# The rows of gathers between two waits of GpSimd: three rows of five against one of seven and one of eight

## The chip, the core and the metric

The kernel runs on one core of a Trainium2 chip. Its time is the device time of one launch in microseconds (us). The engines are PE (TensorE), with its weight loads as PEld, DVE (VectorE), ACT (ScalarE), POOL (GpSimd) and SP (SyncE, which only issues transfers here). Each has its own instruction stream; they meet in semaphores alone.

## What is computed

A recommendation tower for 2048 samples. Each sample has 32 ids, one per field; each id picks a row of 16 f32 values out of its field's table. The products of every pair of the 32 rows are summed to 496 numbers, 16 dense values are appended, and a small network follows:

```python
e = jnp.stack([tbl_0[ids[:, 0]], ..., tbl_31[ids[:, 31]]], axis=1)
z = jnp.sum(e[:, row, :] * e[:, col, :], axis=2)      # all pairs row < col
h = jnp.concatenate([z, dense_ctx], axis=1)
h = jnp.maximum(h @ W_top1 + b_top1, 0.0)             # 512 x 512
h = jnp.maximum(h @ W_top2 + b_top2, 0.0)             # 512 x 256
y = h @ W_top3
```

Seventeen tables have 1000 or 1250 rows; fifteen have 12,500 or 125,000.

## The kernel before

The samples go in 16 tiles of 128, one sample per partition. For the 17 small tables PE looks the rows up: a one-hot matrix times the table, split in three bf16 parts, in six rounds for each tile; DVE picks the result out of PSUM (`pick`, line 470). The one-hots come from ACT (`distances` at line 844, `onehots` at line 854), out of a block of group numbers, `gids`, which SP loads for each tile as a broadcast to 128 partitions (line 297, 17 x 128 f16 values or 4352 bytes in each partition).

The 15 large tables can't be looked up so. For them POOL issues 15 gathers per tile (line 367), each an indirect DMA that brings one field's row of 16 values for all 128 samples. The fields stand in three groups of 7, 5 and 3, and each group has a semaphore for even and one for odd tiles, `landed[g][t % 2]`; every gather adds 16 to it when its data has landed.

In its window for tile t, DVE

- multiplies the small fields among themselves (`small_products`, line 480),
- waits for group 0 and multiplies its 7 fields with the 17 small ones (line 489, 128x1904), and then with each other (line 498),
- waits for group 1 and does the same (line 489, 128x1920), and sums part of the products (line 517),
- waits for group 2 (line 489, 128x1392, and line 508) and sums the rest (line 517).

Between these it does the six picks of tile t+1. PE sums the first 384 pairs by transposes (line 663), turns what DVE has summed (line 670) and runs the network for tiles t-1 and t-2 (lines 683, 692 and 699), with ACT's copies between its steps (line 882 is the copy of z to SBUF, which is layer 1's input).

What sets the order around the change:

- POOL's stream is written out, with no loop. It first builds a few constants, and then does nothing but the 240 gathers and their waits. From tile 2 on, POOL may write a group of tile t only after DVE has used the same group of tile t-2 (semaphore `made`).
- POOL also waits for its own gathers. The 15 fields of a tile are numbered 0 to 14 (`place`), and after places 4, 9 and 14 it waits until the gathers of that group issued so far have landed, before it issues the next one. In the last tile there is no such wait.
- SP's stream is a chain of waits: for tile t it waits until ACT has used the `gids` of tile t-1, loads those of tile t+1 (line 297), waits until the z of tile t-2 is complete in PSUM, and loads the dense values of tile t (line 301). So the next load of `gids` also stands behind that wait for z.

The loops of DVE, PE, ACT and SP take two tiles in one round; tiles 0, 1, 14 and 15 are written apart.

Of the kernel before, what the change touches and what calls it, by code (L numbers as in the profile page):

```python
# [28 lines left out]
S = len(SMALL)  # L29
# [23 lines left out]
GROUPS = [7, 5, 3]  # L53
GROUP_AT = [S + sum(GROUPS[:g]) for g in range(len(GROUPS) + 1)]

RUN = 5

SHIFTS = (S - 1) // 2
CIRCLES = [(GROUPS[0] - 1) // 2, (GROUPS[1] - 1) // 2, 0]
# [55 lines left out]
def dlrm_tower(nc, dense, ids, small_ids, ids_dram, tables, w1, b1, w2, b2, w3, out):  # L115
    with ExitStack() as ctx:
# [3 lines left out]
        def sem(name):  # L120
            return ctx.enter_context(nc.semaphore(name))
# [91 lines left out]
        landed = [[sem(f"landed{g}_{i}") for i in range(2)] for g in range(len(GROUPS))]  # L213
# [42 lines left out]
        LAST_TILE = TILES - 1  # L256

        def steps_done(t, step):
            return STEPS * t + step + 1
# [78 lines left out]
        @block.gpsimd  # L338
        def _(pool):
            nc.gpsimd.iota(row_int[:], pattern=[[1, 1]], base=0, channel_multiplier=1).then_inc(iotas_made, 1)  # L340
            nc.gpsimd.iota(cand_int[:], pattern=[[1, SLOTS]], base=0, channel_multiplier=0).then_inc(iotas_made, 1)
            nc.gpsimd.iota(field_int[:], pattern=[[1, TENS], [0, SLOTS]], base=0, channel_multiplier=0
                           ).then_inc(iotas_made, 1)
            nc.gpsimd.iota(place_int[:], pattern=[[1, TENS * SLOTS]], base=0, channel_multiplier=0
                           ).then_inc(iotas_made, 1)
            nc.gpsimd.memset(ident[:], 0.0).then_inc(ident_zeroed, 1)
            pool.wait_ge(ident_zeroed, 1)
            nc.gpsimd.affine_select(out=ident[:], in_=ident[:], compare_op=ALU.not_equal, fill=1.0, base=0,
                                    pattern=[[-1, P]], channel_multiplier=1).then_inc(ident_ready, 1)

            pool.wait_ge(first_ids_loaded, 16)
            for t in range(TILES):
                if t == 1:
                    pool.wait_ge(ids_loaded, 16)
                for g, n in enumerate(GROUPS):
                    if t >= 2:

                        pool.wait_ge(made, steps_done(t - 2, GROUP_STEPS[g]))
                    for i in range(n):
                        f = FIELDS[GROUP_AT[g] + i]  # L360
                        at = (PLACES[g] + i) * D
                        done = landed[g][t % 2]
                        if t == LAST_TILE:
                            for k, (group, first, count) in enumerate(LAST_PIECES):
                                if group == g and first <= i < first + count:
                                    done = last_landed[k]
                        nc.gpsimd.indirect_dma_start(  # L367
                            emb[:, t, at:at + D], None, tables[f],
                            bass.IndirectOffsetOnAxis(ap=idx[:, t, f:f + 1], axis=0)
                        ).then_inc(done, 16)  # L370
                        place = GROUP_AT[g] + i - S
                        if t < LAST_TILE and place % RUN == RUN - 1:
                            pool.wait_ge(done, 16 * (t // 2 * n + i + 1))

        @block.vector
        def _(dve):
# [653 lines left out]
```

## Time and profile before

| | us |
|---|---|
| time, median of 3 runs | 390.6 (388.05 to 390.77) |
| time of the profiled execution | 392.31 |
| its span, first to last instruction | 390.5 |
| PE busy | 301.6 (77%) |
| DVE busy | 248.0 (63%) |
| POOL busy | 227.9 (58%) |
| ACT busy | 145.0 (37%) |

The mean granted clock of TensorE was 0.921. The times of launches are what is compared; the span is the part of a launch that the trace shows. A row of the timeline gives start, duration, engine, line, operation, output and input, the count where rows were merged, and in brackets how long the engine had been idle before it and what ended that idle time ("issue" is nothing that the profile shows). The bar of POOL's row ends where it has written out the gather's work list, not where the data has landed.

### The profile page before, as it was taken

The numbers are of one execution on the slowest core, as the hardware profiler recorded it, in microseconds if no ns is written. First come the engines' busy times: TensorE is split into PE (matmuls) and PEld (weight loads), VectorE is DVE, ScalarE is ACT, GpSimd is POOL, SyncE is SP. The second block draws the span as 40 slices with busy tenths as digits, with TensorE's granted clock in tenths as the row PEclk, the third lists the DMA queues.
The fourth block names the chain that finished last, engine by engine and source line by source line (L and its number), as shares of the span: only waits on it lengthen the run. The fifth ranks groups of instructions, "written<-read, shape, count | busy, mean of one in ns | idle before, by whom it ended". The sixth has DMA issues, their size and how long they took to land.

```text
span 390.5 us, 7439 instructions
## 1 busy us (share of the span) xinstructions
PE 301.6 (77%) x2748; PEld 278.9 (71%) x2748; DVE 248.0 (63%) x326; ACT 145.0 (37%) x311; POOL 227.9 (58%) x250
## 2 busy tenths in 40 slices
PE   1658697999777967977796797879679786978377
PEld 1348696888776857977785797768579776877366
DVE  6798769565956567394647739464673946556541
ACT  3982443434442424344242434424243441113012
POOL 6446655566656656665665666566566656657700
PEclk9988899899998999889899988989998898999759
DMA  6770020202020200102030110202012000000000
GB/s 140 207 236 5 8 64 6 65 6 64 8 63 5 64 6 15 53 6 63 5 64 6 24 44 6 63 6 64 6 17 51 6 6 5 7 8 6 7 3 1
DMA packets 19036, 14.51 MB, mean 37 GB/s; under 512 B 9727, under 2 KB 16461, under 8 KB 19022
## 3 DMA queue, kind: packets, MB, share of 16 engines
q1 hardware_dynamic: 10284, 11.69, 9.9%
q0 software_dynamic: 7680, 1.98, 6.5%
q10 hardware_dynamic: 1058, 0.66, 0.6%
q8 instruction: 8, 0.13, 0.2%
q14 instruction: 6, 0.05, 0.0%
HBM read 14.24 MB, written 0.08 MB: 37 GB/s over the span
## 4 chain that ended last, share of the span: by engine, by line
POOL 24%; PE 24%; issue 20%; DMA 11%; DVE 7%; another core or an unknown queue 6%; ACT 6%; SPq 1%; POOLq 0%; DVEq 0%; ACTq 0%
POOL emb L367 24%; DMA emb<-tbl,idx 10%; PE bank L663 7%; PE bank L683 6%; PE bank L645 5%; DVE emb L470 2%; PE bank L642 2%; ACT distance L844 2%; PE bank L780 1%; DVE prod L480 1%; DVE prod L489 1%; PE bank L692 1%; PE bank L699 1%; DVE mask L438 1%
## 5 line engine op out<-in xcount | busy, mean ns | idle before, releaser
L367 POOL DMA_INDIRECT emb<-tbl,idx x240 | 226.7, 945 | 141.8 <-DMA emb<-tbl,idx 80.1
L489 DVE TENSOR_TENSOR prod<-emb,bank 128x1904 f32<-128x1904 f32 (+5 forms) x51 | 94.5, 1854 | 99.3 <-DMA emb<-tbl,idx 97.3
L663 PE MATMUL bank<-ident,prod 128*128 128x128 f32 x768 | 101.9, 286 | 11.6 <-issue 4.5
L663 PEld LDWEIGHTS bank<-ident,prod 128*128 128x128 f32 x768 | 94.1, 197 | 14.3 <-issue 5.7
L683 PE MATMUL bank<-zT,w_sb 128*128 128x128 f32 x480 | 73.4, 303 | 17.7 <-ACT zT L882 16.5
L645 PE MATMUL bank<-parts,onehot 125*128 125x160 bf16 (+1 forms) x816 | 84.8, 239 | 1.8 <-issue 1.7
L683 PEld LDWEIGHTS bank<-zT,w_sb 128*128 128x128 f32 x480 | 65.9, 213 | 21.5 <-issue 19.8
L645 PEld LDWEIGHTS bank<-parts,onehot 125*128 125x128 bf16 x816 | 68.0, 104 | 1.2 <-issue 0.7
L642 PE MATMUL bank<-far_ten,named_ten 100*128 100x160 bf16 x160 | 40.9, 256 | 36.1 <-issue 26.6
L470 DVE TENSOR_REDUCE emb<-bank 128x480 f32 (+5 forms) x96 | 52.6, 583 | 10.3 <-remote 4.3
L875 ACT COPY bank<-emb 128x112 f32 (+3 forms) x32 | 7.8, 243 | 107.7 <-issue 68.4
L642 PEld LDWEIGHTS bank<-far_ten,named_ten 100*128 (+1 forms) x160 | 17.1, 107 | 42.8 <-issue 34.7
L888 ACT ACTIVATE h1T<-bank,b_sb 128x128 f32<-128x128 f32 x60 | 21.5, 362 | 57.4 <-PE bank L683 33.7
L480 DVE TENSOR_TENSOR prod<-bank,emb 128x2176 f32<-128x2176 f32 x16 | 38.7, 2418 | 5.6 <-ACT bank L868 5.5
L517 DVE TENSOR_REDUCE z_last<-prod 128x22 f32<-128x352 f32 (+3 forms) x32 | 34.8, 1087 | 2.2
L854 ACT ACTIVATE onehot<-distance,one 125x1152 bf16<-125x1152 bf16 (+1 forms) x30 | 35.7, 1194 | 0.0
L844 ACT ACTIVATE distance<-gids,minus_row 125x1152 bf16<-125x1152 f16 (+1 forms) x30 | 34.4, 1193 | 0.5 <-DMA gids<-small_ids_f 0.3
L692 PE MATMUL bank<-h1T,w_sb 128*128 128x128 f32 x240 | 31.6, 287 | 2.0 <-ACT h1T L888 1.8
L692 PEld LDWEIGHTS bank<-h1T,w_sb 128*128 128x128 f32 x240 | 29.7, 201 | 2.5 <-issue 2.4
L642 PE MATMUL bank<-far_eight,named_eight 70*128 70x128 bf16 x112 | 24.7, 221 | 7.4 <-DVE emb L470 4.7
L882 ACT COPY zT<-bank 128x512 f32<-128x512 f32 x15 | 8.8, 583 | 31.6 <-remote 30.6
L498 DVE TENSOR_TENSOR prod<-bank,emb 128x336 f32<-128x336 f32 (+1 forms) x32 | 13.2, 412 | 9.1 <-ACT emb L877 7.8
(71 smaller groups left out, 137.4 us busy)
## 6 DMA issues: line engine op xcount, KB each, us to landing
gids<-small_ids_f SPq DMA_DIRECT2D x16, 544.0 KB
emb<-tbl,idx POOLq DMA_INDIRECT x240
w_sb<-w SPq DMA_DIRECT2D x1, 1024.0 KB
w_sb<-w SPq DMA_DIRECT2D x1, 512.0 KB
tab<-tbl SPq DMA_DIRECT2D x7, 56.0 KB
tab<-tbl SPq DMA_DIRECT2D x5, 70.0 KB
tab<-tbl ACTq DMA_DIRECT2D x5, 70.0 KB
z_last<-dense SPq DMA_DIRECT2D x16, 8.0 KB
```

The source lines that it names most:

```text
L367: nc.gpsimd.indirect_dma_start(emb[:, t, at:at + D], None, tables[f], bass.IndirectOffsetOnAxis(ap=idx[:, t, f:f + 1], axis=0)).then_inc(d ...
L470: nc.vector.tensor_reduce(emb_at(t, SMALL_PLACE + first, n).rearrange("p a x -> p (a x)"), bank[:, from_bank, 0:width_of(r)].rearrange("p ...
L480: nc.vector.tensor_tensor(prod[:, 0:PAIR_AT[1] * D].rearrange("p (k x) -> p k x", k=SHIFTS), strided(bank[:, E_BANK, 0:S * D], [[0, SHIFTS ...
L489: return nc.vector.tensor_tensor(prod[:, at * D:(at + n * a) * D].rearrange("p (j i d) -> p j i d", j=n, d=D), strided(emb_at(t, PLACES[g] ...
L517: nc.vector.tensor_reduce(z_last[:, place, first - SUM_AT:end - SUM_AT], prod[:, first * D:end * D].rearrange("p (a d) -> p a d", d=D), AX ...
L642: nc.tensor.matmul(look, named[0:rows, bass.ts(t, P)], far[0:rows, field * w:(field + 1) * w], start=True, stop=False)
L645: mm = nc.tensor.matmul(look, onehot[:, place, i, :], parts[:, k, CAND_AT[i] * D:CAND_AT[i + 1] * D], start=False, stop=(k == PARTS - 1))
L663: mm = nc.tensor.matmul(bank[:, Z_BANK + place, c * P:(c + 1) * P], v[:, d, :], ident[:], start=(d == 0), stop=(d == D - 1), is_transpose= ...
L683: mm = nc.tensor.matmul(bank[:, H1_BANK + n % 2, 0:P], w1_sb[:, c, n * P:(n + 1) * P], zT[:, place, c, :], start=(c == 0), stop=(c == CHUN ...
L692: mm = nc.tensor.matmul(bank[:, H2_BANK, m * P:(m + 1) * P], w2_sb[:, c, m * P:(m + 1) * P], h1T[:, c, :], start=(c == 0), stop=(c == H1 / ...
L844: nc.scalar.activation(distance[:, first * P:(first + n) * P].rearrange("p (f j n) -> p f j n", f=n, n=SUB), gids[0:ROWS, place, :].rearra ...
L854: nc.scalar.activation(onehot[:, place, first:first + n, :].rearrange("p f b -> p (f b)"), distance[:, first * P:(first + n) * P], ACT.Rel ...
```

## The change

POOL waits for landings twice in a tile: after the 7 gathers of group 0, and after the 8 gathers of groups 1 and 2, where it waits for group 2. The gathers themselves, their order and their semaphores are as before, and so are the waits for DVE and the last tile.

```diff
-RUN = 5
+ROW_ENDS = (0, 2)
...
                         ).then_inc(done, 16)
-                        place = GROUP_AT[g] + i - S
-                        if t < LAST_TILE and place % RUN == RUN - 1:
-                            pool.wait_ge(done, 16 * (t // 2 * n + i + 1))
+                    if t < LAST_TILE and g in ROW_ENDS:
+                        pool.wait_ge(landed[g][t % 2], 16 * n * (t // 2 + 1))
```

POOL's stream from tile 0's first gather to tile 1's last, before. `landed0_0` is group 0's semaphore for even tiles, `landed2_1` group 2's for odd ones; a row "x4" is four gathers with no wait.

```order
L367 DMA emb<-tbl,idx 128x16 [waits first_ids_loaded]
L367 DMA emb<-tbl,idx 128x16 x4
L367 DMA emb<-tbl,idx 128x16 [waits landed0_0]
L367 DMA emb<-tbl,idx 128x16 x4
L367 DMA emb<-tbl,idx 128x16 [waits landed1_0]
L367 DMA emb<-tbl,idx 128x16 x4
L367 DMA emb<-tbl,idx 128x16 [waits ids_loaded,landed2_0]
L367 DMA emb<-tbl,idx 128x16 x4
L367 DMA emb<-tbl,idx 128x16 [waits landed0_1]
L367 DMA emb<-tbl,idx 128x16 x4
L367 DMA emb<-tbl,idx 128x16 [waits landed1_1]
L367 DMA emb<-tbl,idx 128x16 x4
```

The same place of POOL's stream after the change, up to the first gather of tile 2.

```order
L367 DMA emb<-tbl,idx 128x16 [waits first_ids_loaded]
L367 DMA emb<-tbl,idx 128x16 x6
L367 DMA emb<-tbl,idx 128x16 [waits landed0_0]
L367 DMA emb<-tbl,idx 128x16 x7
L367 DMA emb<-tbl,idx 128x16 [waits ids_loaded,landed2_0]
L367 DMA emb<-tbl,idx 128x16 x6
L367 DMA emb<-tbl,idx 128x16 [waits landed0_1]
L367 DMA emb<-tbl,idx 128x16 x7
L367 DMA emb<-tbl,idx 128x16 [waits made,landed2_1]
```

The wait inside group 1 is gone, the one inside group 0 has moved behind that group's seventh gather, and the one at the tile's end has stayed. No other engine's stream has changed.

## Rows read from the trace of the kernel before

**Rows 1.** The page's busy times, and its chain that ended last by engine

```profile
PE 301.6 (77%) x2748; PEld 278.9 (71%) x2748; DVE 248.0 (63%) x326; ACT 145.0 (37%) x311; POOL 227.9 (58%) x250
...
POOL 24%; PE 24%; issue 20%; DMA 11%; DVE 7%; another core or an unknown queue 6%; ACT 6%; SPq 1%; POOLq 0%; DVEq 0%; ACTq 0%
```

**Rows 2.** Waits, longest in total: engine, line, releaser, total us, times, longest

```profile
DVE prod L489 <- DMA emb<-tbl,idx: 97.3, 25, 5.5
POOL emb L367 <- DMA emb<-tbl,idx: 80.1, 44, 5.2
```

**Rows 3.** Timeline of POOL, tile 9 from its first gather to tile 10's first

```profile
215.25 0.94 POOL L367 DMA_INDIRECT emb<-tbl,idx  x1 [1.63 <-DMA emb<-tbl,idx]
...
220.24 0.94 POOL L367 DMA_INDIRECT emb<-tbl,idx  x1 [0.30 <-issue]
222.87 0.95 POOL L367 DMA_INDIRECT emb<-tbl,idx  x1 [1.69 <-DMA emb<-tbl,idx]
...
230.47 0.94 POOL L367 DMA_INDIRECT emb<-tbl,idx  x1 [1.64 <-DMA emb<-tbl,idx]
...
238.01 0.94 POOL L367 DMA_INDIRECT emb<-tbl,idx  x1 [1.61 <-DMA emb<-tbl,idx]
```

**Rows 4.** Timeline of POOL, first and last of the last tile's 15 gathers

```profile
352.11 0.94 POOL L367 DMA_INDIRECT emb<-tbl,idx  x1 [1.59 <-DMA emb<-tbl,idx]
...
369.59 0.94 POOL L367 DMA_INDIRECT emb<-tbl,idx  x1 [0.30 <-issue]
```

**Rows 5.** Timeline of POOL, early rows: starts of tiles 1 to 4, and two more

```profile
4.40 0.94 POOL L367 DMA_INDIRECT emb<-tbl,idx  x1 [0.30 <-issue]
...
21.91 0.94 POOL L367 DMA_INDIRECT emb<-tbl,idx  x1 [5.17 <-DMA emb<-tbl,idx]
...
29.53 0.94 POOL L367 DMA_INDIRECT emb<-tbl,idx  x1 [1.58 <-DMA emb<-tbl,idx]
...
53.59 0.94 POOL L367 DMA_INDIRECT emb<-tbl,idx  x1 [3.05 <-DMA emb<-tbl,idx]
...
77.72 0.94 POOL L367 DMA_INDIRECT emb<-tbl,idx  x1 [2.98 <-DMA emb<-tbl,idx]
...
101.15 0.94 POOL L367 DMA_INDIRECT emb<-tbl,idx  x1 [1.78 <-DMA emb<-tbl,idx]
```

**Rows 6.** Timeline of DVE: small products and group 1 of tiles 3 and 4

```profile
86.09 2.42 DVE L480 TENSOR_TENSOR prod<-bank,emb 128x2176 f32<-128x2176 f32 x1 [3.29 <-ACT bank L868]
...
97.21 2.15 DVE L489 TENSOR_TENSOR prod<-emb,bank 128x1920 f32<-128x1920 f32 x1 [2.08 <-DMA emb<-tbl,idx]
...
105.60 2.42 DVE L480 TENSOR_TENSOR prod<-bank,emb 128x2176 f32<-128x2176 f32 x1
```

**Rows 7.** Timeline of DVE: group 1 of tile 8, groups 0 and 1 of 9, group 0 of 15

```profile
211.36 2.15 DVE L489 TENSOR_TENSOR prod<-emb,bank 128x1920 f32<-128x1920 f32 x1 [2.73 <-DMA emb<-tbl,idx]
...
227.32 2.14 DVE L489 TENSOR_TENSOR prod<-emb,bank 128x1904 f32<-128x1904 f32 x1 [5.01 <-DMA emb<-tbl,idx]
...
234.21 2.15 DVE L489 TENSOR_TENSOR prod<-emb,bank 128x1920 f32<-128x1920 f32 x1 [3.28 <-DMA emb<-tbl,idx]
...
362.04 2.14 DVE L489 TENSOR_TENSOR prod<-emb,bank 128x1904 f32<-128x1904 f32 x1 [4.17 <-DMA emb<-tbl,idx]
```

**Rows 8.** Timeline of SP's queue: three of the issues of `gids`

```profile
49.25 0.43 SPq L297 DMA_DIRECT2D gids<-small_ids_f  x1
...
222.87 0.43 SPq L297 DMA_DIRECT2D gids<-small_ids_f  x1
...
291.24 0.43 SPq L297 DMA_DIRECT2D gids<-small_ids_f  x1
```

**Rows 9.** Stretches: length, busy PE, PEld, DVE, ACT, POOL (count), granted clock, DMA share, GB/s

```profile
215.20:238.00 22.80, 18.28 (x166) 16.87 (x165) 14.20 (x17) 8.41 (x19) 14.15 (x15) 0.90 0.15 30
50.00:52.50 2.50, 2.50 (x31) 2.49 (x30) 2.07 (x3) 1.78 (x5) 0.54 (x1) 1.00 0.70 224
223.50:226.50 3.00, 3.00 (x15) 2.17 (x15) 0.00 (x0) 1.31 (x3) 2.21 (x3) 0.50 0.65 193
```

## Prediction, made before the changed kernel had run

> **What bounds the kernel now.** I read the page's busy shares and its chain first. PE is busiest, and the chain names PE as often as POOL [rows 1]; neither settles it, since a share is an average and the chain mixes stages. The waits say more: DVE loses 97.3 us waiting for gathers to land, and POOL 80.1 us waiting for its own [rows 2]. So I followed POOL alone.
>
> The timeline of tile 9 [rows 3] shows how POOL lives. Within a row of gathers the next one starts 1.25 us after the last (0.94 us of bar and 0.30 us idle). Across a wait it is more: 2.63 us from 220.24 to 222.87, with 1.69 us idle. From tile start to tile start, 215.25 to 238.01, pass 22.76 us, which is twelve short steps and three long ones: 12 x 1.249 + 3 x 2.59. All its idle time stands in front of landings. From tile 4 to tile 15 there are eleven such tiles in 251 us (101.15 in [rows 5] to 352.11 in [rows 4]), so the beat is POOL's for two thirds of the kernel. In the same tile PE is busy 18.3 of 22.8 us and DVE 14.2 [rows 9], and DVE stands idle 5.0 and 3.3 us until group 0 and group 1 land [rows 7]. In the last tile it stands idle 4.17 us for group 0, so there too the end hangs on POOL. From the last tile's first gather to the end of the span is 390.5 - 352.11 = 38.4 us.
>
> **The first tiles are different.** Up to tile 3 POOL is ahead and DVE and PE set the pace: DVE first waits noticeably for group 1 in tile 3, for 2.08 us [rows 6]. POOL's own early waits are irregular: 5.17 us idle before 21.91, while the weights load, 3.05 us before 53.59 and 2.98 us before 77.72, where the usual is 1.6 [rows 5].
>
> **The change, part by part.**
>
> *One landing wait less in each of tiles 0 to 14.* A long step becomes a short one: 2.59 - 1.25 = 1.34 us. A tile is then 13 x 1.249 + 2 x 2.59 = 21.4 us. Over 15 tiles that is 20 us, all on POOL, which sets the pace.
>
> What a longer row does to the landing behind it no long row with a wait shows; the last tile bounds it. Its 15 gathers follow each other without a wait in 17.48 us, 1.249 us a step [rows 4], so POOL isn't held up by gathers still under way. And DVE reads group 0 of that tile at 362.04, 2.44 us after the seventh gather's start (352.11 + 6 x 1.249 = 359.60) [rows 7]; after a row with a wait it reads group 1 2.49 us after its last gather (230.47 + 1.25 = 231.72, read at 234.21). So I take 2.59 us for the long step. The bounds: 1.25 (the landing costs nothing) to 6.1, the step that ended at 21.91.
>
> The Trainium skill, "DMA: Bandwidth & Descriptors", section on the anatomy of one DMA on GpSimd's path, puts a fixed cost of about 2.0 us on each, issue to semaphore. By that figure a long step would be about 2.0, the wait removed worth 0.8 us and the sum over 15 tiles about 11 us instead of 20. The trace shows the long step whole, at 2.6, so the trace decides.
>
> *The wait inside group 0 moves behind its seventh gather.* For DVE this is good: group 0's last gather starts 7.5 us after the tile's first instead of 8.9 (224.12 - 215.25). Group 1's starts at 7.5 + 2.6 + 4 x 1.25 = 15.1 instead of 16.5. POOL's waits for DVE (`made`, two tiles back) cost nothing: DVE reads a group as soon as it has landed in the bound tiles, and a lead of two tiles, some 43 us, is never reached in the sum below.
>
> *But it moves into another transfer.* Once per tile the broadcast of `gids`, 544 KB, fills the DMA engines: 0.65 and 0.70 of their time in the stretches 223.5 to 226.5 and 50.0 to 52.5, against 0.15 on average [rows 9]. It starts about 1 us after SP issues it [rows 8]. In tile 9 SP issues at 222.87, 11.5 us after DVE began group 1 of tile 8 (211.36, [rows 7]); the issue hangs on the z of the tile before, so I take this distance as fixed. After the change, group 1 is read at 15.1 + 2.45 = 17.55 in its tile, SP issues at 29.05, which is 7.65 in the next tile of 21.4. The seventh gather of group 0 starts at 7.5: POOL now waits for exactly the gather that meets the broadcast. Before, it met places 5 and 6, for which POOL didn't wait. If the landing is late, the next group 1 and the next broadcast are late by as much, so the meeting repeats.
>
> What does one cost? Nearest rows: the gather started 0.35 us after SP's issue (49.60, where the issue is at 49.25) ended in 3.05 us idle, 1.4 more than usual. The one started 1.25 us after it (224.12) was read by DVE at 227.32, after 3.20 us instead of 2.45: 0.75 more. Mine starts 0.15 us before the issue. I take 1.2 us, between them and nearer the first; bounds are 0 (it gets through before the broadcast's start) and 2.5 (it waits for the whole of it, by the length of the stretch). `gids` is last issued at 291.24, in POOL's tile 12.
>
> **The sum, POOL's starts of tiles.** Tile 0: seventh gather at 4.40 + 5 x 1.25 = 10.6, a long step of 3.1 (tables still load), eighth of the second row at 22.4, then a step of 4.1 (my choice between 2.6 and 6.1, as the weights are nearly in by then): tile 1 at 26.6 instead of 29.53. Then three clean tiles of 21.4, as the broadcasts of that time are set by the slower DVE and PE; the one issued at 49.25 [rows 8] falls just after tile 2's first gather at 48.0, and I assume that the next two miss the waits nearly as well (0.3 us for both): tile 4 at 91.1 instead of 101.15. That is 10 us gained, 5.4 by four waits and the rest by the irregular ones that are not met again.
>
> Now POOL leads. DVE could have started group 1 of tile 3 at 97.21 - 2.08 = 95.1. How fast DVE and PE go when nothing is late the trace bounds: small products of tile 3 to those of tile 4 take 19.5 us with 2.08 of landing in it [rows 6]. I take 19 us a tile, so group 1 of tile 7 is ready at 171, and POOL's lands at 91.1 + 3 x 21.4 + 17.5 = 172.8: POOL sets the pace again from tile 7. Broadcasts meet the waited gather in tiles 8 to 12, five times 1.2 = 6.0 us. Tile 15 starts at 91.1 + 11 x 21.4 + 6.0 = 332.5, against 352.11: 19.6 us gained. With the same 38.4 us behind it the span is 370.9. The profiled execution took 392.31, 1.7 above the median of the runs, so I subtract from the median: 390.6 - 19.6 = **371 us**.
>
> **The rivals.**
>
> - *No meeting.* The broadcast comes 1 us later than I place it or the gather slips through. Then 6 us more are gained: 365. For it: the rows bound the cost at zero; against: in tile 9 the places beside it, 5 and 6, started at 222.87 and 224.12, right at the issue at 222.87 [rows 3, 8].
> - *Meetings at full price and more often.* 1.4 to 1.75 us in eight tiles is 11 to 14 us: 376 to 379.
> - *DVE and PE can't follow.* Between reading group 1 and group 0 of the next tile DVE had 227.32 - 211.36 = 16.0 us, of which 5.0 idle; now 13.8. PE has little idle time too, 4.5 us of 22.8, and some of it is waiting for ACT. If their beat were 22 us, group 1 of tile 15 would come at 95.1 + 12 x 22 = 359, and the span ends 20.9 us later (390.5 less 369.6, where it came before): 380.
> - *Slower.* The seventh gather, in the engines' queues just as the broadcast enters, is held for all of its 2.5 us in each of the twelve tiles that have one. That gives back 30 us of 25.6: 395. It decides from 2.1 us per tile. Against it: the nearest gather lost 1.4.
> - *Nothing happens.* POOL's waits were cover for another bound and its freed time turns into a wait of another engine: 390. DVE's idle time in front of every landing speaks against it.
>
> **Chances.** Forecast 0.50, no meeting 0.18, full price 0.13, DVE and PE 0.11, nothing 0.04, slower 0.04. The range from 364 to 379 takes in the first three and the unknown prices and leaves out about 2 in 10. A difference under 1% can't be told from none here: faster by over 1% 0.92, within 1% 0.04, slower by over 1% 0.04.
>
> **What would show it.** POOL's waits should fall from 44 to 29, with short steps still at 1.25 us inside rows of seven and eight; were they longer there, the first part is wrong. The wait at a tile's end should be 1.6 us idle everywhere after tile 1. The wait behind group 0 should be 1.6 in tiles without a meeting and some 2.8 in tiles 8 to 12, with SP's issue of `gids` 0.1 to 0.2 us after the seventh gather's start; a steady 1.6 there is the first rival. Tile 4 should start near 91 and tile 15 near 332. DVE should still stand idle before groups 0 and 1 in the late tiles; if it doesn't, DVE and PE have become the bound. And from the last tile's first gather to the end should be 38 us: if much more, the tail wasn't POOL's.

## The result and the profile after

The changed kernel took **479.0 us** in the median of its runs (476.77 to 483.17), against 390.3 before: 1.230 times as long [1.220, 1.240]. I had forecast 371. Some runs of a kernel fall into a slower group; medians here are of all its runs, ratios and intervals of the faster runs alone. The profiled execution took 480.3 us, its span was 478.4 at a mean granted clock of 0.81, where before it was 390.5 at 0.92.

The page of the changed kernel, its busy times and the chain by engine (before: [rows 1]):

```profile
PE 354.2 (74%) x2748; PEld 312.8 (65%) x2748; DVE 249.4 (52%) x326; ACT 145.8 (30%) x311; POOL 228.0 (48%) x250
...
PE 62%; issue 16%; another core or an unknown queue 12%; ACT 3%; DVE 3%; SPq 2%; DMA 1%; DVEq 0%; ACTq 0%
```

POOL, a quarter of the chain before, is gone from it. PE has 62%, and is "busy" 53 us longer for the same 2748 matmuls. Its longest waits (before: [rows 2]):

```profile
ACT h1T L887 <- remote: 115.8, 19, 10.3
ACT emb L859 <- DVE emb L469: 98.9, 15, 8.1
DVE emb L469 <- remote: 93.0, 26, 7.9
POOL emb L367 <- DVE prod L488: 93.0, 12, 9.5
...
POOL emb L367 <- DMA emb<-tbl,idx: 34.2, 18, 4.4
```

POOL's waits for its own landings did fall, from 80.1 us to 34.2. A new one took their place: POOL now waits 93.0 us for DVE to set the buffer of two tiles back free. ACT and DVE wait for "remote" (a releaser that the profile doesn't find), at the lines that read what PE has written. Starts of rows in POOL's timeline of the changed kernel (before: [rows 3 to 5]):

```profile
99.97 0.94 POOL L367 DMA_INDIRECT emb<-tbl,idx  x1 [4.43 <-DVE prod L488]
110.03 0.94 POOL L367 DMA_INDIRECT emb<-tbl,idx  x1 [1.62 <-DMA emb<-tbl,idx]
...
128.95 0.94 POOL L367 DMA_INDIRECT emb<-tbl,idx  x1 [9.25 <-DVE prod L488]
...
412.76 0.94 POOL L367 DMA_INDIRECT emb<-tbl,idx  x1 [9.23 <-DVE prod L488]
```

Tile 4 starts at 99.97 and tile 15 at 412.76, a tile every 28.4 us; a landing wait in mid tile is the usual 1.6. So POOL has its rows as planned and isn't the bound. What is, the timeline of PE, ACT, DVE and POOL shows inside one row of eight gathers (248.92 to 258.6) and behind it:

```profile
248.85 2.06 PE L682 MATMUL bank<-zT,w_sb 128*128 128x128 f32 x8 [0.44 <-issue]
...
253.17 0.27 PE L682 MATMUL bank<-zT,w_sb 128*128 128x128 f32 x1 [1.03 <-issue]
...
253.90 0.27 PE L682 MATMUL bank<-zT,w_sb 128*128 128x128 f32 x1 [0.45 <-issue]
...
254.62 0.56 PE L682 MATMUL bank<-zT,w_sb 128*128 128x128 f32 x1 [0.46 <-issue]
...
256.03 0.59 PE L682 MATMUL bank<-zT,w_sb 128*128 128x128 f32 x2 [0.85 <-issue]
...
257.45 0.59 PE L682 MATMUL bank<-zT,w_sb 128*128 128x128 f32 x2 [0.83 <-issue]
...
260.33 0.62 ACT L887 ACTIVATE h1T<-bank,b_sb 128x128 f32<-128x128 f32 x2 [8.17 <-remote]
...
261.69 2.42 DVE L479 TENSOR_TENSOR prod<-bank,emb 128x2176 f32<-128x2176 f32 x1 [5.74 <-ACT bank L867]
...
268.06 0.94 POOL L367 DMA_INDIRECT emb<-tbl,idx  x1 [9.46 <-DVE prod L488]
```

The later matmuls at L682 need nothing that isn't there: between them PE stands idle with the releaser "issue", and they start 0.7 to 1.4 us apart, where elsewhere eight of them take 1.06 us. It begins 4 us into the row of gathers and ends 2 us after it. ACT stands idle 8.17 us for a product of L682, DVE 5.74 us for ACT, and POOL's next tile waits 9.46 us for DVE. I call this **PE's crawl**, and a matmul that starts 0.55 to 1.6 us after the one before a slow step. The trace of before has 31 such steps, that of the changed kernel 125; PE is idle under "issue" before 16 and 117 of them.

Slow steps are only a part of it. The first product that ACT waits for is made by the eight matmuls that end at 250.91, before the first slow step of this row. The semaphore that they raise is updated, by the trace's semaphore events, at 260.30, **9.4 us later** and 1.7 us after the last gather's bar, and ACT starts at 260.33. So PE's semaphores come late too, and that is why the profile finds no releaser and writes "remote".

### The profile page after: what moved, and what is told of

It is laid out like the page before. It is cut to its first block, busy times and chain, and to the rows that moved or that the text cites. A ratio compares the mean times of both kernels' runs of the same rounds, so it can differ in the third digit from the quotient of the medians.

```text
span 478.4 us, 7452 instructions
## 1 busy us (share of the span) xinstructions
PE 354.2 (74%) x2748; PEld 312.8 (65%) x2748; DVE 249.4 (52%) x326; ACT 145.8 (30%) x311; POOL 228.0 (48%) x250
## 4 chain that ended last, share of the span: by engine, by line
PE 62%; issue 16%; another core or an unknown queue 12%; ACT 3%; DVE 3%; SPq 2%; DMA 1%; DVEq 0%; ACTq 0%
PE bank L662 19%; PE bank L682 14%; PE bank L644 13%; PE bank L691 8%; PE bank L641 5%; PE bank L698 2%; DVE prod L488 1%; DVE emb L469 1%; SPq L288 1%; DMA tab<-tbl 1%; PE bank L779 1%; PE bank L669 1%; SPq L289 1%; ACT onehot L853 1%
## 5 line engine op out<-in xcount | busy, mean ns | idle before, releaser
L662 PE MATMUL bank<-ident,prod 128*128 128x128 f32 x768 | 125.5, 317 | 21.7 <-issue 18.2
L662 PEld LDWEIGHTS bank<-ident,prod 128*128 128x128 f32 x768 | 109.2, 202 | 31.5 <-issue 28.1
L644 PE MATMUL bank<-parts,onehot 125*128 125x160 bf16 (+1 forms) x816 | 99.4, 249 | 29.7 <-issue 29.6
L682 PE MATMUL bank<-zT,w_sb 128*128 128x128 f32 x480 | 83.1, 311 | 34.3 <-issue 24.5
L682 PEld LDWEIGHTS bank<-zT,w_sb 128*128 128x128 f32 x480 | 72.9, 222 | 38.7 <-issue 30.0
L644 PEld LDWEIGHTS bank<-parts,onehot 125*128 125x128 bf16 x816 | 71.8, 108 | 37.9 <-issue 36.8
L641 PE MATMUL bank<-far_ten,named_ten 100*128 100x160 bf16 x160 | 43.3, 271 | 13.6 <-ACT onehot L853 5.5
L691 PE MATMUL bank<-h1T,w_sb 128*128 128x128 f32 x240 | 39.3, 328 | 5.6 <-issue 3.5
L691 PEld LDWEIGHTS bank<-h1T,w_sb 128*128 128x128 f32 x240 | 37.0, 241 | 7.5 <-issue 4.3
L859 ACT COPY emb<-emb (+1 forms) x16 | 4.8, 298 | 98.9 <-DVE emb L469 98.9
L641 PEld LDWEIGHTS bank<-far_eight,named_eight 70*128 (+1 forms) x112 | 10.9, 97 | 6.0 <-issue 5.1
```

The costliest lines, as they stand in the source:

```text
L641: nc.tensor.matmul(look, named[0:rows, bass.ts(t, P)], far[0:rows, field * w:(field + 1) * w], start=True, stop=False)
L644: mm = nc.tensor.matmul(look, onehot[:, place, i, :], parts[:, k, CAND_AT[i] * D:CAND_AT[i + 1] * D], start=False, stop=(k == PARTS - 1))
L662: mm = nc.tensor.matmul(bank[:, Z_BANK + place, c * P:(c + 1) * P], v[:, d, :], ident[:], start=(d == 0), stop=(d == D - 1), is_transpose= ...
L682: mm = nc.tensor.matmul(bank[:, H1_BANK + n % 2, 0:P], w1_sb[:, c, n * P:(n + 1) * P], zT[:, place, c, :], start=(c == 0), stop=(c == CHUN ...
L691: mm = nc.tensor.matmul(bank[:, H2_BANK, m * P:(m + 1) * P], w2_sb[:, c, m * P:(m + 1) * P], h1T[:, c, :], start=(c == 0), stop=(c == H1 / ...
```

## The experiments

They ran on four chips, called A to D here, because the chips turned out to differ: on B and C PE crawls, on A and D it doesn't; the chip of the first result isn't known, and its traces look like those of B and C. The ratios are to the kernel before on the same chip in the same hour. "Tile 15" is the start of its first gather, "tail" what follows it to the end of the span, both us of the profiled execution.

| kernel, rows of gathers in a tile | chip | median us | ratio | slow steps | tile 15 | tail |
|---|---|---|---|---|---|---|
| before (as first profiled), 5 5 5 | - | 390.3 | | 31 | 352.1 | 38.4 |
| changed (as first profiled), 7 8 | - | 479.0 | 1.230 | 125 | 412.8 | 65.7 |
| row15, 15 | A | 337.5 | 0.865 | 13 | 306.1 | 29.7 |
| rows744, 7 4 4 | A | 390.5 | 1.000 | 7 | 360.5 | 28.4 |
| pause, 5 5 5 | A | 387.3 | 0.992 | 5 | 355.5 | 28.6 |
| before_again, 5 5 5 | B | 402.6 | 1.002 | 73 | 348.9 | 51.1 |
| after_again, 7 8 | B | 484.0 | 1.196 | 146 | 419.4 | 62.3 |
| rows69, 6 9 | B | 483.2 | 1.203 | 145 | 415.6 | 62.9 |
| nowait, all in one | B | 500.8 | 1.248 | 141 | 432.5 | 63.9 |
| after_third, 7 8 | C | 478.2 | 1.206 | 129 | 407.8 | 64.9 |
| row15_again, 15 | C | 485.5 | 1.239 | 136 | 420.8 | 63.3 |
| after_fourth, 7 8 | B | 482.4 | 1.191 | 135 | 414.3 | 66.6 |
| rows744_again, 7 4 4 | B | 427.5 | 1.058 | 87 | 363.3 | 65.9 |
| pause_again, 5 5 5 | B | 395.1 | 0.977 | 34 | 355.8 | 37.4 |
| after_fifth, 7 8 | D | 364.2 | 0.933 | 11 | 332.1 | 29.9 |
| row15_third, 15 | D | 340.1 | 0.872 | 12 | 309.6 | 29.6 |

The kernel before took 390.1 us on A, 403 and 410 on B in two hours (means of 401.3 and 404.5 in the runs that the ratios use), 392.7 on C and 389.9 on D. The ratios of after_again and after_third are of two runs each and without an interval. On A and D none of the few slow steps stands under "issue": they are ordinary waits.

**Where the landing is awaited.** Every one of these kernels is the kernel before with one line changed, the places after which POOL waits:

```
-                        if t < LAST_TILE and place % RUN == RUN - 1:
+                        if t < LAST_TILE and place in (6, 10, 14):
                             pool.wait_ge(done, 16 * (t // 2 * n + i + 1))
```

That is rows744; row15 has `place == 14`, rows69 `place in (5, 14)`, and nowait leaves out both lines. In pause the landing isn't awaited but a write of 1.6 us:

```
+                        if t < LAST_TILE and place in (4, 9, 14):
+                            nc.gpsimd.memset(pause[:], 0.0).then_inc(paused, 1)
+                            pool.wait_ge(paused, 3 * t + place // 5 + 1)
```

> POOL waits for landings only at the end of each tile (one row of 15 gathers). Theory A (PE gets its instructions done only at one matmul per 0.7 to 1.4 us from about 5 us after the start of a row of gathers until some 1.5 us after its end): each tile has about 14 us of such crawl, so the tiles take over 30 us and the kernel over 500 us; the crawl begins 5 us into each row. Theory B (what slows PE is tied to where group 0's landing is awaited, for instance the seventh gather meeting the gids broadcast): that wait is gone, so the kernel is no slower than the changed one, 479 us, and rather near 370.

> Three waits per tile as before the change, but after places 6, 10 and 14: rows of 7, 4 and 4. POOL's own beat stays 22.8 us. Theory A: one crawl per tile of about 4 us (row of 7), none in the rows of 4; PE has 4.5 us to spare in a tile, so the time is 390 to 410 us. Theory C (PE is slow because POOL has run ahead of DVE and all engines meet in a worse phase, not because of the rows' length): POOL can't run ahead with three waits, 390 us, and no matmuls 0.7 us apart inside the row of 7.

> Rows of 5, 5 and 5 as before the change, but between two rows POOL doesn't wait for a landing: it writes zeros to 128x1792 f32 values (1 to 2 us) and waits for that alone. The kernel does nothing else differently. If a break in POOL's gathers is what PE needs, the time is near 390 us or less, moved by 45 times the difference of the two breaks. If it needs the landing (no gather under way), PE crawls as in the changed kernel: over 450 us.

On chip A, row15 took 337.46 us, ratio 0.865 [0.860, 0.869]: two landing waits less in a tile gain 52 us. Two tile starts in its timeline of POOL and the stretch of a tile (columns as in [rows 9]):

```profile
246.17 0.95 POOL L367 DMA_INDIRECT emb<-tbl,idx  x1 [1.59 <-DMA emb<-tbl,idx]
...
266.20 0.94 POOL L367 DMA_INDIRECT emb<-tbl,idx  x1 [1.61 <-DMA emb<-tbl,idx]
```

```profile
249.00:269.05 20.05, 16.56 (x170) 15.61 (x170) 14.05 (x17) 8.33 (x19) 14.17 (x16) 1.00 0.15 34
```

The tile takes 20.03 us, which is 14 short steps and one long one (14 x 1.249 + 2.54). PE does its 170 matmuls in 16.6 us, at full clock: here it can follow, and POOL is the bound throughout. rows744 is 1.000 [0.996, 1.003] and pause 0.992 [0.989, 0.994]. As many waits cost as much wherever they stand, and a break of 1.6 us without any landing costs about what the landing did. All of this spoke for my sum and against the result.

> The kernel before, unaltered, once more. Its time stays 390, since POOL's landing waits set its beat with or without a crawl of PE. Theory D: PE's semaphores come at the ends of its matmuls, as they do in the trace of one row of 15, and not up to 4 us behind them, as in the first trace of this kernel. Theory E: they come late again.

> The changed kernel, unaltered, once more. One row of 15 took 337 us and showed no crawl of PE (matmuls 0.7 us apart); the changed kernel's trace shows one in nearly every row. Theory D (the crawl belongs to the circumstances of those executions, not to the rows): its tiles now take POOL's 21.4 us, 360 to 372 us, no crawl. Theory E (it belongs to this program): 479 us again, crawl from tile 0 on.

> Two waits per tile like the change, but after places 5 and 14, rows of 6 and 9. Theory E with a cause in the program's layout: either clean or crawling, no telling which; if clean, POOL's beat of two waits gives 21.4 us a tile and 360 to 372 us. Theory D: 360 to 372 us. A cause in the waits themselves (two waits per tile): 479 us.

> No landing wait at all. POOL's beat would be 15 x 1.249 = 18.7 us a tile, 1.34 less than one row of 15 with its wait (337 us): 317 us if DVE and PE follow. PE is busy about 17 to 18 us of each tile, so they may not: 317 to 337 us. If landing waits hold PE's crawl off, it comes back here and the time is over 400 us.

On chip B the same kernel before gave 402.6 (1.002 [0.995, 1.009]), and the changed one 484.0 again. rows69 took 483.2 (1.203 [1.193, 1.213]) and nowait 500.8 (1.248 [1.237, 1.259]): with two breaks in a tile 483 and 484, with none 501. A seventh gather that meets the broadcast isn't the cause, since rows69 and nowait wait for another gather or for none. And the result repeats.

What before_again was to show of PE's semaphores came out as "late again". In the traces of A and D every update of a semaphore that PE raises, but for 7 in some 273, stands within 0.06 us of a matmul's end. On B it is 80 of 256 for the kernel before, and in the changed kernel's first trace 137 of 263. And rows of five aren't free of the crawl there: the kernel before has slow steps under "issue" in 27 of its 45 rows of five, 54 in all.

> The changed kernel again, beside one row of 15 on the same chip. So far the two stand on different chips: 337 us for one row of 15 on one where the kernel before took 390.1, and 484 us for the changed kernel on one where it took 403.4. Theory D (a chip, or its surroundings, lets PE crawl while POOL gathers, another does not): if the trace here has no crawl, 360 to 372 us; if it has, 475 to 490 us. Theory E (it is this program): 475 to 490 us whatever the other kernels do.

> One row of 15 again, on the same chip as the changed kernel. Theory D: both clean (337 us beside 360 to 372) or both crawling (470 to 510 us beside 480). Theory E: 337 us beside 480.

Chip C decided between "the changed kernel has something of its own" and "the chips differ". row15, 337 us on A, took **485.5** here, 1.239 [1.226, 1.253]. Lines of its PE, waiting for nothing, in a row of 12 gathers (250.83 to 265.5, the rest of a tile's 15 after POOL had waited 4.83 us for DVE) and just behind it:

```profile
262.89 0.29 PE L642 MATMUL bank<-far_ten,named_ten 100*128 100x160 bf16 x1 [1.64 <-issue]
...
265.03 0.29 PE L645 MATMUL bank<-parts,onehot 125*128 125x160 bf16 x1 [1.12 <-issue]
...
267.15 0.29 PE L645 MATMUL bank<-parts,onehot 125*128 125x160 bf16 x1 [1.56 <-issue]
```

**The crawl by itself.** pe_small and pe_big keep only PE, in a loop of equal matmuls, beside rows of gathers of several lengths on POOL:

```
+            with pe.Fori(0, TICKS) as j:
+                for k in range(PER_TICK):
+                    mm = nc.tensor.matmul(bank[:, k % 4, 0:P], weights[:], moving[:, 0:P], start=True, stop=True)
+                mm.then_inc(ticks, 1)
```

> Nothing of the tower is computed (the output is zeros). PE runs 56 rounds of 32 f32 matmuls 128x128 with no wait at all; meanwhile POOL issues rows of 3, 5, 7, 10 and 15 gathers, a row of 15 plain 8 KB loads and 15 writes of zeros, each row after a fixed count of PE's rounds and with its landings awaited. On a chip with the crawl: matmuls 0.7 us apart or more from about 5 us into the rows of 7, 10 and 15, none in the row of 3, no crawl in the writes of zeros; the plain loads tell whether it is the gathers' work or any DMA of POOL. On a chip without: 0.115 us a matmul throughout.

> The same with 16 bf16 matmuls of 512 columns per round, about half as many PE instructions per us. If what runs short is something spent per instruction of PE, the crawl starts later in a row (after 9 us or more) or is gone; if it is time that PE's data path loses, it starts at the same 5 us. On a chip without the crawl: even throughout.

In pe_small (a matmul each 0.112 us) rows of 3 and 5 gathers lose nothing; a row of 7 loses 0.8 us, one of 10 3.9, one of 15 10.1 (the time between matmuls beyond 0.112, summed over the gaps of 0.339 and more). Fifteen plain transfers and fifteen writes on POOL lose nothing. The writes last 15 us, but the plain transfers only 8.0, a little less than the row of 7 gathers, which has just one slow step. What tells there is PE's semaphore, raised after every 32 matmuls: in pe_small it comes 0.014 us after the matmul's end nearly everywhere, also 6.6 us into the plain transfers, but **3.60 us** late when the matmul ends 6.4 us into the row of 7 gathers, 5.63 and 3.56 in the rows of 10 and 15, and 0.79 behind the row of 5. So gathers hold up PE's semaphores before any matmul is late. (In the loop only the recorded event tells it; in the kernel ACT really starts that late.) Its stretches (PE, PEld, DVE, POOL, clock, DMA share, GB/s): without a row, the first 9 us of the row of 15, its rest, and what follows:

```profile
26.00:34.00 8.00, 8.00 (x74) 8.00 (x73) 0.00 (x0) 0.00 (x0) 1.00 0.01 1
...
186.70:195.00 8.30, 8.30 (x76) 8.30 (x76) 0.00 (x0) 6.47 (x7) 1.00 0.10 6
195.00:208.00 13.00, 6.09 (x29) 4.33 (x27) 0.00 (x0) 7.71 (x9) 0.72 0.08 6
208.00:216.00 8.00, 8.00 (x59) 8.00 (x60) 0.00 (x0) 0.00 (x0) 0.82 0.00 0
```

For 9 us PE runs as if alone, then 13 us give it 29 matmuls in place of 116. The granted clock falls in that stretch, to 0.72, and is still 0.82 in the next, after PE has stood half idle. It is 1.00 until 200.7, 4.9 us after the first slow step began, and then 0.50, the lower of its two levels, for 10 us; so it follows the crawl and doesn't make it.

```profile
196.58 1.00 PE L163 MATMUL bank<-moving,weights 128*128 128x128 f32 x5 [0.51 <-issue]
198.72 1.00 PE L163 MATMUL bank<-moving,weights 128*128 128x128 f32 x4 [1.13 <-issue]
200.86 0.78 PE L163 MATMUL bank<-moving,weights 128*128 128x128 f32 x2 [1.14 <-issue]
202.27 0.37 PE L163 MATMUL bank<-moving,weights 128*128 128x128 f32 x1 [0.63 <-issue]
```

The first late matmul stands 8.9 to 9.2 us after the row's start, behind 80 to 82 matmuls, in each of the three rows, in the row of 7 just after the last gather's bar. pe_big's matmuls last 0.216 us: rows up to 10 lose nothing, and in the row of 15 the first slow step comes after 17.6 us, again behind **82 matmuls** (2.1 us lost in its three slow steps). So in these loops what sets the beginning is a number of PE's matmuls since the gathers began, not time and not gathers. The number isn't the same in the whole kernel: in row15_again the first slow step of a tile stands behind 56 to 68 matmuls in 14 of the 15 places where there is one. What else counts there isn't shown.

The DMA engines are nearly idle in it (share 0.08), so this is no lack of bandwidth. The Trainium skill, "Runtime: NRT & Kernel Launch", section on instruction fetch mechanics, says that an engine's sequencer streams its program in blocks over a DMA queue of its own; starved of them, PE would look like this, I think. No trace here bears it out: pe_small's queue of instructions moved one packet in the whole 428 us, and the changed kernel's moved 15 where the kernel before had 14.

**What breaks it off.** pe_breaks is pe_small with six rows of 15 gathers: without a break; the landing awaited after every 5; a write of 1.5 us after every 5; the write after each; the landing after each; and the landing after every 7.

```
+                    if every and i % every == every - 1:
+                        if rest == "land":
+                            pool.wait_ge(landed, 16 * issued)
+                        else:
+                            nc.gpsimd.memset(wide[:], 0.0).then_inc(written, 1)
+                            wrote += 1
+                            pool.wait_ge(written, wrote)
```

> Nothing of the tower is computed (zeros are put out). PE as in pe_small. POOL issues six times 15 gathers: in one row; landing awaited after every 5; 1.5 us of writing zeros after every 5; the same write after each gather; landing awaited after each; landing awaited after every 7. With the crawl, if a reserve of about 80 matmuls is used up by gathering and restored in breaks: crawl in the first from 8.6 us on, little or none where a break comes every 5, none where one comes after each, and short crawls in the last. If the number of gathers counts whatever the breaks, all six crawl alike. Without the crawl: even throughout.

> Rows of 7, 4 and 4 with three waits. On a chip without the crawl 390 us as measured. On one with it: pe_small lost nothing in rows of 3 and 5 and little in the row of 7, from 8.6 us after its start; the tower's PE issues faster in its lookups and crawled from 5 to 6 us. One row of 7 per tile costs about 4 us of PE, which has 4.5 to spare: 390 to 410 us. If breaks don't restore what the row uses up, over 450 us.

> Rows of five with a write of zeros between them in place of the landing wait, on whatever chip comes. Without the crawl 387 us as measured. With it: if the break in POOL's gathering restores PE's reserve, 385 to 405 us, like the kernel before on that chip; if only an empty gather queue does, 450 us or more.

> The changed kernel on whatever chip comes. Row of 15 and changed kernel crawled together (485 and 478 us), so theory E is out. Theory D: where PE does not crawl this takes 360 to 372 us, POOL's beat of 21.4 us a tile; where it does, 470 to 490 us.

The stretches of pe_breaks (columns as above): the unbroken row's first 9 us and its rest, landing after every 5, write after every 5:

```profile
21.70:30.80 9.10, 9.10 (x84) 9.10 (x82) 0.00 (x0) 6.97 (x8) 1.00 0.05 5
30.80:43.00 12.20, 5.30 (x22) 3.69 (x21) 0.00 (x0) 7.29 (x8) 0.72 0.06 6
83.30:104.10 20.80, 20.80 (x188) 20.80 (x188) 0.00 (x0) 14.12 (x15) 1.00 0.06 6
140.50:161.60 21.10, 21.10 (x191) 21.10 (x190) 0.00 (x0) 16.90 (x17) 1.00 0.06 5
```

Lost: 10.0, 0, 0, then 0, 0, and 5.0 with the landing after every 7, again from 82 matmuls on, and in the second seven already from 25. A break of POOL's gathering of about 1.6 us is enough to keep this loop's matmuls going if it comes every 5 gathers; it need not be a landing. Every 7 is too late. PE's semaphores are 0.8 to 1.7 us late even with breaks every 5, and on time only with one after each gather. Nothing in the loop's PE waits for them, but the kernel's ACT and DVE do.

The whole kernel on B goes the same way. rows744 has the kernel before's three waits, and one row of seven: 427.5 us, 1.058 [1.047, 1.069], where on A it was 1.000. I had expected 390 to 410: the row of seven isn't the only one that crawls, 21 of its slow steps under "issue" stand in rows of four. pause, with breaks every 5 that await no landing, took 395.1, **0.977 [0.971, 0.982]**, and 0.992 on A. So it is a little faster than the kernel before on either kind of chip, and faster than the changed one only where PE crawls. It has 11 slow steps under "issue" in its 44 rows of five; that breaks every five keep PE quite free in the whole kernel isn't so. rows744_again at the row of seven that starts at 212.64, PE's timeline:

```profile
218.26 0.61 PE L683 MATMUL bank<-zT,w_sb 128*128 128x128 f32 x4 [0.38 <-issue]
...
219.67 0.51 PE L683 MATMUL bank<-zT,w_sb 128*128 128x128 f32 x3 [0.81 <-issue]
...
221.83 0.23 PE L645 MATMUL bank<-parts,onehot 125*128 125x160 bf16 x1 [0.47 <-issue]
222.53 0.42 PE L645 MATMUL bank<-parts,onehot 125*128 125x160 bf16 x2 [0.47 <-issue]
```

after_fourth repeated the result beside them: 482.4, 1.191 [1.184, 1.199].

**The changed kernel where PE doesn't crawl.** dve_small, on the same chip, puts 1792 small copies on DVE in place of PE's matmuls.

> The changed kernel once more, beside the kernel before. On a chip on which PE is held up in long rows: 470 to 487 us, as in the three earlier runs. On a chip like the first one, where a whole tile's gathers in one row took 337 us: 360 to 372 us, my original sum, as PE then follows.

> One landing wait per tile. 337 us where PE is not held up, 480 to 490 where it is; it tells the two kinds of chip apart by itself, and with the run of the changed kernel whether both kernels change sides together.

> The tower is left out and the output is not the reference's: PE has no work, and DVE runs 1792 small copies (128x4, near 0.06 to 0.1 us each) one after the other, while POOL issues rows of 3, 5, 7, 10 and 15 gathers, then 15 plain transfers and 15 writes. Theory A (what runs short is counted per instruction of an engine, whichever engine it is): after about 80 copies from the start of a long row DVE too goes down to one in 0.7 us or more, until 2 to 3 us after the row, and the row of 15 loses 5 us or more. Theory B (it is PE's alone): DVE loses nothing in any row, below 0.3 us. If this chip is one on which PE is not held up either, only a loss would say something; the run of the changed kernel beside it tells which kind of chip it is.

On chip D the changed kernel took **364.2 us**, 0.933 [0.927, 0.939], and row15 340.1. Both change sides together. In the changed kernel's trace there, waits, three tile starts of POOL's timeline with the landing wait that was longest, and SP's issue before that one:

```profile
DVE prod L488 <- DMA emb<-tbl,idx: 94.5, 28, 4.2
...
POOL emb L367 <- DMA emb<-tbl,idx: 53.0, 28, 3.2
```

```profile
92.97 0.94 POOL L367 DMA_INDIRECT emb<-tbl,idx  x1 [1.62 <-DMA emb<-tbl,idx]
...
200.51 0.94 POOL L367 DMA_INDIRECT emb<-tbl,idx  x1 [1.61 <-DMA emb<-tbl,idx]
...
212.11 0.94 POOL L367 DMA_INDIRECT emb<-tbl,idx  x1 [3.17 <-DMA emb<-tbl,idx]
...
332.06 0.94 POOL L367 DMA_INDIRECT emb<-tbl,idx  x1 [1.58 <-DMA emb<-tbl,idx]
```

```profile
207.37 0.44 SPq L297 DMA_DIRECT2D gids<-small_ids_f  x1
```

dve_small shows no slow step in any row of gathers: from each row's first gather to its last DVE makes 13.6 copies per us, and 14.1 between rows, so some 3% less all along (0.6 us in the row of 15), and there no copy starts over 0.14 us after the one before; DVE's semaphores are on time. But it ran on D, where PE loses nothing either, so whether the crawl is PE's alone stays open.

## Why the prediction was wrong

- **The sum for POOL was right, and it is what the kernel does on a chip without the crawl.** On D tile 4 starts at 92.97 (predicted 91.1) and tile 15 at 332.06 (predicted 332.5); 28 landing waits (29), short steps 1.25. Even the meeting is there: in tile 9 SP issues `gids` at 207.37, the seventh gather starts at 208.0, and its landing costs 3.17 us idle instead of 1.6. In tiles 8 to 12 the meetings cost 0.3, 1.6, 0.1, 1.2 and 0.8, 4.0 in all where I had 6.0.
- **The step that failed is "how fast DVE and PE go when nothing is late: 19 us a tile".** Where PE crawls they go at 28.4 us a tile. Against my span of 370.9: tile 4 comes 8.9 later (99.97 to 91.1), tiles 4 to 15 take 312.8 instead of 241.4, 71.4 more, and the tail is 65.7 instead of 38.4, 27.3 more. That is 107.6, and the span is 107.5 longer. None of it is POOL's own time.
- **The rival "DVE and PE can't follow" had the right engine and the wrong size.** I let their beat go from 19 to 22, by adding up busy time. (Its 380 rests on a misread row as well: 369.6 is the start of the last gather [rows 4], while DVE reads group 1 of tile 15 at 365.84 and 368.25, which would make it 381 to 384.) No busy share of the kernel before tells what PE does inside a row longer than five, since such a row stands only in its last tile.
- **That row was there to be read, and I read only POOL and DVE in it.** The timeline of the kernel before, last tile, whose 15 gathers run to 370.5:

```profile
360.39 1.95 PE L683 MATMUL bank<-zT,w_sb 128*128 128x128 f32 x16
...
367.70 0.37 PE L663 MATMUL bank<-ident,prod 128*128 128x128 f32 x1 [0.98 <-issue]
...
369.10 0.37 PE L663 MATMUL bank<-ident,prod 128*128 128x128 f32 x1 [1.02 <-issue]
...
371.20 0.37 PE L663 MATMUL bank<-ident,prod 128*128 128x128 f32 x1 [1.03 <-issue]
...
373.37 0.63 ACT L888 ACTIVATE h1T<-bank,b_sb 128x128 f32<-128x128 f32 x2 [8.74 <-remote]
```

  Five slow steps from 366.4 on, three of them shown, and an ACT wait of 8.74 us for "remote", ACT's longest, in the one long row the kernel had. ACT waits for the sixteen matmuls at L683, which end at 362.34; their semaphore comes at 373.34, 2.8 us after the gathers. My 38.4 us of tail held it already: where nothing crawls the tail is 28.4 to 29.9. "The tail moves as it is" was thus 8.5 us too long for chip D, which is why the span there is 361.9 (332.06 + 29.9) and not 370.9: the smaller meetings (2 us less) and tile 4's later start (1.9 us more) cancel. The whole gain on D, 389.9 to 364.2, is 25.7 us where I had 19.6; no trace of the kernel before on D shows where the rest lies.
- **The wait was cover, for something else than I asked.** I gave "slower" one mechanism, a held gather. The landing wait after every fifth gather did nothing for the data; it kept POOL from gathering more than five times in a row, and pause shows that a write of 1.6 us there does the same.
- Each crawl is paid for again through the buffers: ACT late, DVE late, and POOL, which is two tiles ahead, waits 9 us for DVE. A lead that "is never reached in the sum" was reached in 12 places.

What stays open: what PE runs short of. The traces show when (some 80 matmuls into back-to-back gathers in the loops, 56 to 68 in row15_again), how (one matmul in 0.7 to 1.4 us, idle under "issue", its semaphores late before that), until when (1.5 to 3 us after the last gather), and that two of four chips don't have it. Every time here is of an execution that was also recorded, so whether recording is itself what runs short couldn't be told apart, and that rival is a serious one. The records differ between the two kinds of chip just as the times do: on A and D the updates of DVE's semaphores are all but complete (315 to 317), while the first trace of the kernel before has 205 of them, that of the changed kernel 241 and row15_again's 260. Whether an execution that nobody records crawls isn't known.

## What to carry to other kernels

A wait that does nothing for the data can still be what keeps another engine going: before taking it away, look for the one place where the kernel already does without it, and read every engine there, not only the two that the wait connects. A matmul idle under "issue" at even steps of 0.7 us and more, beside a long wait for "remote" on the engine that reads it, is a sign of it. If GpSimd gathers beside a dense TensorE, time long and short rows on more than one chip before believing either: rows of 15 gained 13% on two chips here and lost 24% on a third. Breaks every five gathers, with useful work in them if there is any, were the safe choice on all four, at the price of that gain.

## What the runs showed of the hardware

- While GpSimd issued indirect gathers back to back (one in 1.25 us), TensorE in a plain loop on one chip ran 80 to 82 matmuls at full rate, whether they lasted 0.11 or 0.22 us, and then 29 in 13 us, until 1.5 to 3 us after the row (pe_small, pe_big; the same on a second chip in pe_breaks). A row of 15 lost 10 us of PE; fifteen writes lost none, nor did fifteen plain transfers, whose row was shorter. In whole kernels two of four chips showed it.
- In each row of 7, 10 and 15 gathers of pe_small one semaphore of TensorE fell due, and it came 3.6 to 5.6 us after its matmul's recorded end instead of 0.014, though no matmul was late yet; in fifteen plain transfers one came in time.
- A break of about 1.6 us every five gathers lost the loop nothing, every seven 5.0 us in 15 gathers. In the whole kernel some rows of five crawled still (54 slow steps in before_again).
- The same program, one gather row per tile, took 337 and 340 us on two chips and 485 on a third, while the kernel before differed by 1% between them (390.1, 389.9, 392.7; 403 to 410 on the fourth).
- In pe_small's row of 15 the granted clock was 1.00 until 4.9 us into the crawl, 0.72 over 13 us of it and 0.82 in the 8 us behind it: PE's idle steps cost a second time, through the clock of what follows. The changed kernel's mean was 0.81, on chip D 0.92.
